# Scaling the first layer norm's rows on ScalarE instead of VectorE in a fused decoder layer

## The reference

```python
x = _layernorm(x + attn(x, ...))          # linear attention, 32 heads of 8, relu(q, k, v)
x = _layernorm(x + xattn(x, ctx, ...))    # softmax attention, 16 heads of 16, rotary positions
x = _layernorm(x + ffn(x, ...))           # low rank: 256 -> 64 -> 1024 -> gelu -> 64 -> 256

def _layernorm(x, axis=-1, eps=1e-05):    # no gain, no bias
    m = jnp.mean(x, axis=axis, keepdims=True)
    v = jnp.var(x, axis=axis, keepdims=True)
    return (x - m) / jnp.sqrt(v + eps)
```

## Time and profile before

| | |
|---|---|
| time, three runs | 636.39, 638.66, 632.85 us (median 636.39) |
| span of the profiled execution, first to last instruction | 634.6 us |
| its own time beyond the span | not given apart; the median of the runs lies 1.8 us above the span |
| TensorE busy | 585.9 us, 92% of the span |
| VectorE busy | 457.3 us, 72% |
| ScalarE busy | 302.2 us, 48% |
| GpSimd busy | 283.8 us, 45% |
| TensorE's granted clock, mean | 0.972 of full |
| `norm1` on VectorE | 32 instructions, 39.2 us |

### The profile page before, as it was taken

How to read it: one execution, slowest core, us unless ns; L and a number is a source line. 1 busy time by engine, 2 the same in 40 slices (tenths; PEclk the granted TensorE clock), 3 DMA queues, 4 the chain that set the end, 5 groups by cost and what they waited for, 6 DMA issues and landing times.

```text
span 634.6 us, 12941 instructions
## 1 busy us (share of the span) xinstructions
PE 585.9 (92%) x4352; PEld 401.6 (63%) x4352; DVE 457.3 (72%) x975; ACT 302.2 (48%) x439; POOL 283.8 (45%) x300
## 2 busy tenths in 40 slices
PE   1775999999999999999999999999998969999993
PEld 1764667676767767686868585868674625455561
DVE  5468588888888879797888888888878672244434
ACT  5221445454546363727273635454444526656561
POOL 4745335453636364544545454546443301224334
PEclk9988899999999999999999999999999888999998
DMA  7415100202020101011110102010100000033322
GB/s 266 109 55 153 59 2 10 68 10 68 7 69 13 62 21 54 20 55 46 30 64 11 67 8 66 8 66 8 34 9 18 26 1 18 17 106 119 107 99 100
DMA packets 26031, 33.80 MB, mean 53 GB/s; under 512 B 6552, under 2 KB 12440, under 8 KB 26008
## 3 DMA queue, kind: packets, MB, share of 16 engines
q1 hardware_dynamic: 25240, 33.07, 16.3%
q10 hardware_dynamic: 768, 0.43, 0.3%
HBM read 22.73 MB, written 8.65 MB: 49 GB/s over the span
## 4 chain that ended last, share of the span: by engine, by line
PE 77%; issue 8%; DVE 7%; POOL 4%; ACT 2%; DMA 1%; POOLq 0%; SPq 0%; DVEq 0%; ACTq 0%
PE FR L1001 16%; PE BK L1001 15%; PE BK L1164 11%; PE SC L1147 10%; PE SC L1121 8%; PE FR L1077 4%; PE FR L1069 3%; PE FR L1205 3%; DVE nmax L848 3%; PE FR L1059 3%; PE BK L1175 2%; POOL rs L533 2%; POOL c_fm L538 2%; PE BK L1077 1%; PE SC L1133 1%
## 5 line engine op out<-in xcount | busy, mean ns | idle before, releaser
L848 DVE TENSOR_REDUCE nmax<-SC 128x4 f32<-128x1024 f32 x128 | 150.8, 1217 | 14.1 <-PE SC L1121 14.1
L625 ACT ACTIVATE probs<-SC 128x1024 f32<-128x1024 f32 x128 | 129.3, 1025 | 34.2 <-PE SC L1147 31.0
L1121 PE MATMUL SC<-k_blk,q_grp 96*128 96x512 f16 x256 | 77.0, 394 | 5.5 <-DVE nmax L848 5.5
L1164 PE MATMUL BK<-probs,v_aug 128*32 128x256 f32 x1024 | 81.2, 391 | 0.0
L1147 PE MATMUL SC<-q_grp,k_blk 128*128 128x256 f16 x512 | 75.7, 276 | 0.5 <-ACT probs L625 0.5
L1147 PEld LDWEIGHTS SC<-q_grp,k_blk 128*128 128x128 f16 x512 | 43.7, 99 | 27.2 <-issue 20.2
L439 POOL TENSOR_TENSOR att_fm_l<-att_raw,att_fm_h 128x512 fp32r<-128x512 f32 x16 | 20.5, 1284 | 76.7 <-ACT att_raw L606 76.7
L428 POOL TENSOR_TENSOR k_cos<-k,cos_t 128x512 f16<-128x512 f16 x16 | 18.4, 1152 | 78.3 <-ACT k L587 77.8
L686 ACT ACTIVATE probs<-SC,b_ff 128x512 f32<-128x512 f32 x64 | 39.6, 688 | 24.4 <-PE SC L1326 23.7
L829 DVE TENSOR_SCALAR x_tm<-y,mv,rs 128x256 f32<-128x256 f32 x32 | 39.2, 1265 | 0.8 <-POOL rs L444 0.8
L1164 PEld LDWEIGHTS BK<-probs,v_aug 128*32 128x32 f32 x1024 | 20.4, 108 | 28.8 <-issue 19.4
(11 more groups left out here) (174 smaller groups left out, 1600.6 us busy)
## 6 DMA issues: line engine op xcount, KB each, us to landing
x_fm<-in_x_fm SPq DMA_DIRECT2D x16, 256.0 KB, 2.7
x_tm<-in_x_tm SPq DMA_DIRECT2D x16, 256.0 KB, 2.9
c_fm<-in_c_fm SPq DMA_DIRECT2D x16, 256.0 KB, 3.4
k_blk<-k_rope SPq DMA_DIRECT2D x256, 8.0 KB, 1.8
x_kept<-x2b SPq DMA_DIRECT2D x16, 256.0 KB, 2.1
x_tm<-x_kept SPq DMA_DIRECT2D x16, 256.0 KB, 2.7
out<-c_fm SPq DMA_DIRECT2D x16, 256.0 KB, 2.0
cos_t<-rope_tables SPq DMA_DIRECT2D x1, 896.0 KB
```

What stands on the lines that cost most here:

```text
L625: act.activation(probs[:, j % 4], SC[j % 2][:], ACT.Exp, scale=SCALE).then_inc(s_exp, 1)
L848: dve.tensor_reduce(nmax[:, t, HC * q:HC * q + HC], SC[c % 2][:], AX.X, ALU.max, negate=True).then_inc(s_max, 1)
L1121: mm = pe.matmul(SC[c % 2][:, k:k + 2].rearrange("p h t -> p (h t)"), q_grp[par][0:QR, hd // HG, t * P:(t + 1) * P], k_blk[par][0:QR, hd:h ...
L1164: mm = pe.matmul(BK[q // 2][HP * k:HP * (k + 1), (q % 2) * T:(q % 2 + 1) * T], v_aug[par][:, t, HC * q + k], probs[:, j % 4, k], start=(t ...
```

## The change

Where `norm1` was, VectorE now has `norm1_shift`: one instruction on 128 x 2 elements that makes `mr1 = -mean * rs1`. ScalarE has a new `norm1`: two activations with the function Identity, each with two factors per row, that compute `rs1 * y1 + mr1`. The first waits for `mr1` and for GpSimd's earlier reading of `x1_tm` (`s_x1b`). VectorE's `add1` gets one more wait, for ScalarE to have read the earlier `y1`.

```diff
+            def norm1(n):                                   # ScalarE
+                act.wait_ge(s_mr1, n + 1)
+                wait(act, s_x1b, n)
+                for t in range(TT):
+                    act.activation(x1_tm[:, t], y1[:, t], ACT.Identity, bias=mr1[:, t:t + 1],
+                                   scale=rs1[:, t:t + 1]).then_inc(s_x1, 1)
...
                 if not tail:
+                    norm1(1)
                     ev_x1(1)
...
                     if j == 6 and tail:
                         ev_x2t(b - 1)
+                if linear:
+                    norm1(b + 2)
                 if tail:
                     ev_p(b - 1)
...
             ev_kv1(1, 1)
+            norm1(0)
             ev_x1(0)
...
             def add1(n):                                    # VectorE
                 dve.wait_ge(s_proj_mm, n + 1)
                 dve.wait_ge(s_xb, n + 1)
+                wait(dve, s_x1, 2 * n)
...
-            def norm1(n):
+            def norm1_shift(n):
                 dve.wait_ge(s_rs1, n + 1)
-                wait(dve, s_x1b, n)
-                for t in range(TT):
-                    dve.tensor_scalar(x1_tm[:, t], y1[:, t], mv1[:, t, 0:1], rs1[:, t:t + 1],
-                                      ALU.subtract, ALU.mult).then_inc(s_x1, 1)
+                dve.scalar_tensor_tensor(mr1[:], mv1[:, :, 0], -1.0, rs1[:], ALU.mult, ALU.mult).then_inc(s_mr1, 1)
```

More of the change, by code:

```diff
@@ L145, in build @@
         rs1 = sb("rs1", [P, TT])
+        mr1 = sb("mr1", [P, TT])
         x1_tm = sb("x1_tm", [P, TT, C])
@@ L250, in build @@
         s_rs1, s_rs2, s_rs3 = sem("s_rs1"), sem("s_rs2"), sem("s_rs3")
+        s_mr1 = sem("s_mr1")
         s_xb, s_x1, s_x1b, s_x2, s_x2b, s_y = map(sem, ("s_xb", "s_x1", "s_x1b", "s_x2", "s_x2b", "s_y"))
@@ L911, in step @@
                         if c == 3:
-                            norm1(1)
+                            norm1_shift(1)
                         if c == 4:
@@ L934, in step @@
                 if linear:
-                    norm1(b + 2)
+                    norm1_shift(b + 2)
                 if tail:
@@ L950, in _ @@
             stats1(0)
-            norm1(0)
+            norm1_shift(0)
             shift_constants(0)
```

## The result

The changed kernel takes 637.9 us in the median of 20 runs (636.5 to 643.3), the kernel before 634.3 in the median of 20 runs beside it (631.0 to 639.0). The ratio is 1.0055, with the interval 1.0032 to 1.0078: slower by 3.5 us (2.0 to 4.9), which is within 1%. The forecast was 638.5 us and "no change at 1%", and both hold. The forecast difference of +2.1 us lies at the low end of the interval. The base of the forecast, 636.4 us, was the median of three runs, and twenty runs put it at 634.3. The two profiled spans, 634.6 and 638.8, differ by 4.2 us.

The account below looks back on a forecast made before the run. TensorE was taken to bound the loop. Loop +1.3, step 0's end +1.1, opening's row 0 +1.8 and step 0's row 1 -2.1 sum to +2.1 us; on a base of 636.4 that gives 638.5 us, range 633.5 to 643.5.

Parts of the forecast that it names:

- TensorE bounds the loop; VectorE's relief is worth nothing: Loop steps: TensorE is busy for 30.52 of 30.52 us, so removing VectorE's 2.64 us pair is costed at nothing.
- The scaling pair: ScalarE's two new activations: 0.59 us each, over 0.98 us after the instruction before ends, or 1.18 without overlap.
- rival 3: Loop: ScalarE's two scalings lie fully behind the last exponential, some 0.45 us a step, giving 643.1 us; chance 0.11.
- The small product at 0.2 us: VectorE's new 128 x 2 instruction takes 0.2 us, at most 1.3 beside GpSimd, and costs nothing in the loop.
- the term of row 1: Step 0, row 1: TensorE's transposes start at 57.4 in place of 59.52, a gain of 2.1 us.
- The loop, +0.10 a step: Transposes at the end of steps 1 to 13 slip 0.10 us each, +1.3 us; bounds 0 and +3.4.
- The worked slip of 0.06: Loop step's end: TensorE's transposes can start at 207.25 in place of 207.19; 0.26 us later without overlap on ScalarE.
- Step 0's end, +1.1: After step 0's last exponentials, TensorE's transposes start at 86.25 in place of 85.09: +1.1 us, +1.4 without overlap.
- Row 0, +1.83: Opening: ScalarE's scalings follow the `kv_tm` copy, so the transposes' copy and the projection come 1.83 us later.
- Rival 1: Step 0: TensorE's shorter stand keeps its clock at 2.4 GHz, saving 2.5 us, giving 636.0; chance 0.22.
- Rival 2: Opening: TensorE's longer stand brings a clock drop of its own, +2.5 us, giving 641.0; chance 0.10.
- Rival 4: Loop: VectorE's relief pays through hidden waits, 0.3 us a step, giving 634.6, or the change misbehaves; chance 0.04.

## Why the prediction was right, point by point

**TensorE bounds the loop; VectorE's relief is worth nothing.** Right. VectorE is busy for 24.07 us of a step for 25.54, and the period is longer by the slip. With the pair early and the tile last it is 30.52, as before: a shorter VectorE list brought nothing there.

**The scaling pair.** Right: 596 ns each for 0.59, 0.98 us behind the end of the instruction ahead, the transposes 1.03 behind the exponential's.

The rule that adds and multiplies belong on VectorE, which the prediction set beside rival 3 (the Trainium skill, page "ScalarE: Activation LUTs", rules for kernel authors), does not hold for these shapes beside this GpSimd. VectorE's median instruction takes 1348 ns, the same scaling on ScalarE 596. Where GpSimd is idle, for row 0, VectorE takes 0.41 us, so there the rule holds. The reason is in the rows: in the step of the earlier trace rows VectorE's pair ends at 206.34, 0.15 us behind GpSimd's second instruction (204.86 + 1.33 = 206.19). The Trainium skill, page "SBUF — State Buffer", section "SBUF: two separate sides", says that VectorE and GpSimd share a pair of ports as an exclusive lock. Whichever starts first holds it for its whole instruction, and the other blocks; for VectorE this goes for two inputs from SBUF, which the small product has, or for certain fast modes. By that rule even a tiny instruction waits for the whole of GpSimd's; the trace agrees, by the 1.24 us of the 128 x 2 product beside GpSimd's 1.29, and 0.16 us where it is alone.

**The small product at 0.2 us.** Wrong as a size. The bounds were 0.17 and 1.3, and it takes 1.23 in the loop and 0.99 in step 0, nearer to the upper one. In the loop it is hidden, as costed. In step 0 it is on the path for 0.92, so the term of row 1 was mis-sized by 0.7: -2.1 forecast, -1.35 measured. VectorE's busy time fell by 21.5 us and not by 36 for the same reason. The prediction had named the upper bound, by which row 1 gains only 1.0, and did not use it in step 0, the one place where it counts. TensorE waits 2.39 us for row 1, where 1.6 were forecast and 3.71 stood before.

**The loop, +0.10 a step.** Right in size, +0.094 (13 steps: +1.2 for +1.3), but nearly half of it for another reason, so that this agreement is partly luck. The worked slip of 0.06 is there: 0.05 by the kernel with the tile last. The "little for a weight load that is held" is not what fills the rest; the 8 bytes of the new tile are, 0.04 a step. I had nothing on the rows that pointed to this.

**Step 0's end, +1.1.** Measured +1.16. **Row 0, +1.83.** Measured +1.89. TensorE waits 1.75 and 1.50 us around the transposes, for 1.8 and 1.5 as forecast.

**The sum.** +2.1 forecast, +2.9 by the parts in the profile, the difference being the 0.7 of the small product. The clock adds to this.

**Rival 1 (0.22), the clock drop of step 0 goes:** it did not go, but it was shorter in the profile after. From 57 to 72 us TensorE is at 1.2 GHz for 6.8 us before (mean granted clock 0.77) and for 3.4 us after (0.89). The five kernels with row 1 on VectorE all have 6.8 us there; of the seven with it on ScalarE four have 3.4 and three have 6.8. So a shorter drop goes with the shorter wait in four of seven kernels, each profiled once. **Rival 2 (0.10), a new drop in the opening:** it came in the profiled execution, with +2.68 us between the two rows for the +2.5 forecast. Behind row 1 0.90 came back. In the five profiled kernels with row 0 late on ScalarE the clock is low for 10.2 to 13.7 us from 36 to 57 us; in the seven others for 0 to 6.8. This stretch begins just behind a drop of the kernel before that ends at 36.1 us; counted from 15 to 57 us, all five have 13.7 us and the seven 3.4 to 10.2. So the drop goes with row 0's place, but it also varies between kernels that have the same opening, and each was profiled once. By its time the change stands between the two: 3.5 us, where the sum without the clock is 2.9 and the sum with it 4.7. What it costs in the median run is open. A chance of 0.10 was too low beside rival 1's 0.22: the change made TensorE's wait in the opening longer, and shortened the one in step 0 by less than half.

**Rival 3 (0.11), full cost on ScalarE:** not so; it would need a period of 30.9. One thing said against it was read wrongly: not every pair of neighbours on ScalarE overlaps, since in the step of the earlier trace rows the second part of `ev_p` starts at 207.14, 0.02 us behind the first (206.74 + 0.38). The scalings themselves overlap by 0.11. The run with two more activations shows that it begins right behind the change's own 0.98 us. **Rival 4 (0.04):** nothing for it.

**The base.** The three runs started from are 2.1 us above the median of twenty. The absolute forecast (638.5 for 637.9) is close by luck: its base was too high by 2.1 and its difference too small by 1.4.

## What to carry to other kernels

When work moves to a less busy engine, its price depends on where it stands in that engine's list, and its length counts only beyond the slack at that place: here one set of instructions took 3.5 us more or less by two places in the list, and 0.66 us more at a place without slack cost 0.66 us a step. Look for a place where the engine is idle, or ahead of an instruction whose own result is wanted late enough: here the last exponential could be 0.98 us later without anyone waiting for it in the loop. Split the change by place, since here one row of sixteen carried all of the gain. Measure a slip of under 0.1 us a step by the distance of two equal instructions many steps apart, because a busy share hides it.

## What the runs showed of the hardware that was not expected

- A VectorE instruction of 2 columns takes 0.16 us alone and 1.21 to 1.33 us where it starts within 0.1 us of a GpSimd instruction of 1.3 us; a scaling of 256 columns on ScalarE takes 585 to 601 ns in all 32 cases, whatever GpSimd does.
- 8 bytes more ahead of the tiles that TensorE reads make its loop slower by 0.043 us a step, with the same instructions; 0.025 of it is in twelve matmuls of `x_fm` by `w_q`, 1.44 us for 1.41.
- The granted clock in one stretch of the opening was low for 0 to 13.7 us in twelve kernels, with differences of 3 to 7 us even where the instructions there were the same. Behind the loop, from 480 to 516 us, it was low for 0 to 6.8 us, so two profiled spans can differ for a reason that the change has no part in.
